# Pyramid-pooled attention in split float32: the 110 cells padded to 128 rows, probabilities normalised before the projection

## The reference

```python
qk  = relu(bn(conv1x1(x, qk_w)))      # 512 -> 256 channels
val = relu(bn(conv1x1(x, v_w)))       # 512 -> 512 channels
key, value = psp(qk), psp(val)        # adaptive max pools 1, 3, 6, 8: 110 cells
scores = softmax(query @ key * 256 ** -0.5)     # 4096 positions x 110 cells
y = scores @ value                    # 4096 x 512
out = x + bn(conv1x1(y, out_w))
```

## Time and profile before

| | us |
|---|---|
| median of the runs (3) | 1450.42 |
| the profiled execution | 1452.24 |
| its span | 1450.6 |
| TensorE matmuls busy | 1401.4 (97%) |
| VectorE busy | 967.7 (67%) |
| ScalarE busy | 434.3 (30%) |
| GpSimd busy | 438.0 (30%) |

### The profile page before, as it was taken

How to read it: one execution, slowest core, us unless ns; L and a number is a source line. 1 busy time by engine, 2 the same in 40 slices (tenths; PEclk the granted TensorE clock), 3 DMA queues, 4 the chain that set the end, 5 groups by cost and what they waited for, 6 DMA issues and landing times.

```text
span 1450.6 us, 17388 instructions
## 1 busy us (share of the span) xinstructions
PE 1401.4 (97%) x6029; PEld 1131.5 (78%) x6029; DVE 967.7 (67%) x1745; ACT 434.3 (30%) x597; POOL 438.0 (30%) x263
## 2 busy tenths in 40 slices
PE   7999999999999999999999999999999999999885
PEld 6888888888788887887788877888878887888653
DVE  6545666776666757667576776666766767766776
ACT  4112232233232232332332232332332232232241
POOL 0000123323323323323133323223223323323366
PEclk9999999999999999999999999999999999999987
DMA  5113243443443442443443442443434442442257
GB/s 189 59 58 98 77 171 120 145 174 118 143 171 118 145 172 96 166 170 120 145 145 136 154 168 93 174 163 127 145 127 149 159 174 104 157 174 91 84 205 259
DMA packets 102923, 204.60 MB, mean 141 GB/s; under 512 B 3242, under 2 KB 3282, under 8 KB 102866
## 3 DMA queue, kind: packets, MB, share of 16 engines
q1 hardware_dynamic: 102290, 202.93, 39.6%
q10 hardware_dynamic: 576, 1.05, 0.2%
HBM read 136.86 MB, written 67.11 MB: 141 GB/s over the span
## 4 chain that ended last, share of the span: by engine, by line
PE 85%; DVE 6%; issue 3%; DMA 2%; POOL 2%; ACT 1%; DVEq 0%; POOLq 0%; SPq 0%; ACTq 0%
PE conv_ps L328 22%; PE conv_ps L329 22%; PE conv_ps L330 22%; PE out_ps L352 3%; PE out_ps L353 3%; PE out_ps L354 3%; POOL xo L283 2%; PE score_ps L364 2%; PE score_ps L366 2%; PE score_ps L365 2%; DMA xo<-x 1%; DMA out<-xo 1%; DVE y L673 1%; DVE part L622 1%; PE sum_ps L341 1%
## 5 line engine op out<-in xcount | busy, mean ns | idle before, releaser
L283 POOL TENSOR_TENSOR xo<-y,xo 128x512 f32<-128x512 f32 x256 | 437.1, 1714 | 1009.3 <-DVE y L673 992.4
L328 PE MATMUL conv_ps<-xh,wh 128*128 128x512 f32 x1536 | 601.9, 392 | 0.0
L329 PE MATMUL conv_ps<-xh,wl 128*128 128x512 f32 x1536 | 600.5, 391 | 0.0
L330 PE MATMUL conv_ps<-xl,wh 128*128 128x512 f32 x1536 | 600.3, 391 | 0.0
L605 DVE TENSOR_REDUCE row_max<-conv_ps 128x64 f32<-128x512 f32 (+2 forms) x576 | 289.7, 531 | 280.3 <-ACT q L466 141.0
L328 PEld LDWEIGHTS conv_ps<-xh,wh 128*128 128x128 f32 x1536 | 289.6, 189 | 63.4
L329 PEld LDWEIGHTS conv_ps<-xh,wl 128*128 128x128 f32 x1536 | 290.1, 189 | 62.4
L330 PEld LDWEIGHTS conv_ps<-xl,wh 128*128 128x128 f32 x1536 | 289.5, 188 | 61.3
L478 ACT ACTIVATE e<-score_ps 110x512 f32<-110x512 f32 x60 | 36.1, 601 | 695.0 <-PE score_ps L366 695.0
L673 DVE TENSOR_TENSOR y<-out_ps,rsum 128x512 f32<-128x512 f32 x238 | 161.9, 684 | 1.1
L466 ACT ACTIVATE q<-conv_ps,shift 128x512 f32<-128x512 f32 x128 | 88.2, 689 | 236.6 <-PE conv_ps L330 236.6
(11 more groups left out here) (103 smaller groups left out, 806.0 us busy)
## 6 DMA issues: line engine op xcount, KB each, us to landing
xo<-x SPq DMA_DIRECT2D x64, 1024.0 KB, 5.5
xa<-x SPq DMA_DIRECT2D x63, 1024.0 KB, 7.7
out<-xo SPq DMA_DIRECT2D x63, 1024.0 KB, 4.2
q<-v_w ACTq DMA_DIRECT2D x4, 256.0 KB, 4.9
xa<-x SPq DMA_DIRECT2D x2, 512.0 KB, 6.1
q<-out_w SPq DMA_DIRECT2D x1, 1024.0 KB, 8.4
out<-xo SPq DMA_DIRECT2D x4, 256.0 KB, 2.0
q<-qk_w SPq DMA_DIRECT2D x1, 512.0 KB, 8.4
```

What stands on the lines that cost most here:

```text
L283: nc.gpsimd.tensor_tensor(xt, y[:, m % 2, :], xt, ALU.add).then_inc(out_added, 1)
L328: nc.tensor.matmul(bank(t, c)[:, :], wh[:, k, cols], hi, start=(k == 0), stop=False)
L329: nc.tensor.matmul(bank(t, c)[:, :], wl[:, k, cols], hi, start=False, stop=False)
L330: last = nc.tensor.matmul(bank(t, c)[:, :], wh[:, k, cols], lo, start=False, stop=(k == KC - 1))
```

## The change

The number of matmuls and of bytes moved stays. What differs:

- **Rows.** Keys, values, shift rows, e, sums and projections have ROWS = 128 rows in place of 110. The 18 added rows are set to zero once, by GpSimd; the matrix of ones that sums the cells has zeros in those rows.
- **Order of the arithmetic.** e is split and summed as before (low part now by GpSimd). Then e is multiplied by 1/sum on VectorE (`normalise`), split again (high part ScalarE, low part VectorE), and this p is projected. The projected blocks need no scaling, and VectorE adds the residual itself (`add_out`). The product `scale_out` and GpSimd's `add_residual` are gone. e has three buffers. GpSimd has the low parts of e and q.
- **Order of a step on TensorE.** sums, convolutions 0 to 2, projections 0 and 1, convolution 3, scores, convolution 4, projections 2 and 3, value projection, convolution 5.
- **Order on VectorE.** refine, normalise, pooling of cells, low part of p, keys; values behind the first row pooling.
- **No hardware loop**: every engine's steps are written out.
- **Tail.** Residuals of the last image go to eight places (two of xa, four of q, two of xo). Scores are computed two tiles and sums one tile ahead of the projection.

The core of the diff (on each engine `for s in range(S)` replaces `steps`; `ap = s - NT - 1`, `ac = s - NT`):

```diff
+ROWS = 128
...
-        e = sb("e", [CELLS, 2, TN])
+        e = sb("e", [ROWS, 3, TN])
...
+        def residual(a):
+            if a < LAST:
+                return xo[:, a % 2, :, :]
+            q2 = [q[:, 2 * i:2 * i + 2, :, :].rearrange("p t c n -> p (t c) n") for i in range(4)]
+            return [xa[:, 0, :, :], xa[:, 1, :, :], q2[0], q2[1], xo[:, 0, :, :], xo[:, 1, :, :], q2[2], q2[3]][a - LAST]
...
+            def split_e_lo(a):
+                pool.wait_ge(e_hi, a + 1)
...
+                nc.gpsimd.tensor_tensor(e_l[:, u, :], e[:, u, :], e_h[:, u, :], ALU.subtract).then_inc(e_lo, 1)
...
+            for s in range(S):
+                if s >= NT:
+                    split_e_lo(s - NT)
+                if s >= NT - 1:
+                    split_q_lo(s - (NT - 1))
...
+            def project(a, m):
+                if m == 0:
+                    pe.wait_ge(p_lo, a + 1)
...
+                if ap >= 0:
+                    sums(ap)
+                conv(s, 0)
+                conv(s, 1)
+                conv(s, 2)
+                if ap >= 0:
+                    project(ap, 0)
+                    project(ap, 1)
+                conv(s, 3)
+                if ac >= 0:
+                    scores(ac)
+                conv(s, 4)
+                if ap >= 0:
+                    project(ap, 2)
+                    project(ap, 3)
+                if ac >= 0 and ac % NT == 0:
+                    project_values(ac // NT)
+                conv(s, 5)
...
+            for a in range(LAST, S):
+                if a + 2 < S:
+                    scores(a + 2)
+                if a + 1 < S:
+                    sums(a + 1)
                 for m in range(OC):
+                    project(a, m)
...
+                if ap >= 0:
+                    guess(ap)
+                if s + 1 < S:
+                    split_hi(s + 1, 0)
+                if ap >= 0:
+                    split_p_hi(ap)
+                if s + 1 < S:
+                    split_hi(s + 1, 1)
...
-                nc.vector.tensor_tensor(y[:, m % 2, :], out_bank(b, t, m)[:, :], rsum[:, :], ALU.mult)\
-                    .then_inc(out_scaled, 1)
...
+            def normalise(a):
+                dve.wait_ge(rsum_ready, a + 1)
+                u = a % 3
+                nc.vector.tensor_tensor(e[:, u, :], e[:, u, :], rsum[:, :], ALU.mult).then_inc(p_made, 1)
...
+                xt = residual(a)[:, m, :]
+                nc.vector.tensor_tensor(xt, out_bank(a, m)[:, :], xt, ALU.add).then_inc(out_added, 1)
...
+                if ap >= 0:
+                    refine(ap)
+                    normalise(ap)
+                    if ap % NT == 0:
+                        values_lo(ap // NT)
+                if s >= 1:
+                    pool_cells(s - 1)
+                if ap >= 0:
+                    split_p_lo(ap)
+                if last_of_batch:
+                    finish_keys(ac // NT)
+                pool_rows(s, 0)
+                if last_of_batch:
+                    finish_values(ac // NT)
...
+            for a in range(LAST, S):
+                if a + 1 < S:
+                    refine(a + 1)
+                    normalise(a + 1)
+                add_out(a, 0)
+                add_out(a, 1)
+                if a + 1 < S:
+                    split_p_lo(a + 1)
+                add_out(a, 2)
+                add_out(a, 3)
```

More of the change, by code:

```diff
@@ L144, in psp_attention @@
         rsum_ready = sem("rsum_ready")
+        p_made = sem("p_made")
+        p_hi = sem("p_hi")
+        p_lo = sem("p_lo")
         vo_turned = sem("vo_turned")
@@ L177, in splits_q @@
[L177 to L211, removed]
+        def wait(eng, s, n):
+            if n > 0:
+                eng.wait_ge(s, n)
@@ L239, in _ @@
             sp.wait_ge(w_in[VC - 1], 16)
-            load(0, 1)
+            load(1)
             sp.dma_start(w_raw[:, CC:PAR, :], out_w.rearrange("(m p) c -> p m c", p=P)).then_inc(w_in[VC + 1], 16)
[L243 to L264, removed]
@@ new lines, in _ @@
+            sp.wait_ge(q_lo, LAST + 2)
+            load_residual(LAST + 2)
+            store(LAST - 1)
+            stored(LAST - 2)
+            load_residual(LAST + 4)
+            sp.wait_ge(q_lo, LAST + 4)
+            load_residual(LAST + 3)
+            stored(LAST - 1)
+            load_residual(LAST + 5)
+            store(LAST)
+            sp.wait_ge(q_lo, LAST + 6)
+            load_residual(LAST + 6)
+            store(LAST + 1)
+            sp.wait_ge(q_lo, LAST + 8)
+            load_residual(LAST + 7)
@@ L268, in _ @@
+            for a in range(LAST + 2, S - 1):
+                store(a)
+            for m in range(OC):
+                sp.wait_ge(out_added, (S - 1) * OC + m + 1)
+                sp.dma_start(out_v[B - 1, :, m, (NT - 1) * TN:], residual(S - 1)[:, m, :]).then_inc(y_last, 16)
+            sp.wait_ge(y_last, (NT - 1 + OC) * 16)
         @block.gpsimd
@@ L285, in step @@
[L285 to L295, removed]
+            one = e[:, 0, 0:ROWS]
+            nc.gpsimd.memset(one, 1.0).then_inc(ones_made, 1)
+            pool.wait_ge(ones_made, 1)
+            nc.gpsimd.affine_select(out=one, in_=one, compare_op=ALU.is_ge, fill=0.0, base=CELLS - 1,
+                                    pattern=[[0, ROWS]], channel_multiplier=-1).then_inc(ones_made, 1)
@@ new lines, in split_q_lo @@
+            def split_q_lo(a):
+                pool.wait_ge(q_hi, a + 1)
+                nc.gpsimd.tensor_tensor(q_l[:, a % 2, :, :], q[:, a % NT, :, :], q_h[:, a % 2, :, :], ALU.subtract)\
+                    .then_inc(q_lo, 1)
+            for s in range(S):
+                if s >= NT:
+                    split_e_lo(s - NT)
+                if s >= NT - 1:
+                    split_q_lo(s - (NT - 1))
+            split_q_lo(LAST + 1)
+            split_e_lo(LAST)
+            split_q_lo(LAST + 2)
@@ L331, in conv @@
                 last.then_inc(conv_done, 1)
-            def sums(b, t):
-                wait(pe, e_lo, b, t, 1, 1 - (NT + 1))
-                if t == 1:
-                    pe.wait_ge(vo_made, b)
-                wait(pe, s_r0_made, b, t, 1, (-1 if sum_bank(b, t) is conv_ps[1] else 0) - (NT + 1))
-                u = (t - 1) % 2
-                nc.tensor.matmul(sum_bank(b, t)[:, :], ones[:, :], e_h[:, u, :], start=True, stop=False)
-                nc.tensor.matmul(sum_bank(b, t)[:, :], ones[:, :], e_l[:, u, :], start=False, stop=True)\
-                    .then_inc(sums_done, 1)
@@ L344, in project, with scores @@
-            def project(b, t, m):
-                if m == 0 and t == 1:
-                    pe.wait_ge(vo_lo, b)
-                four = isinstance(b, int) and NT * b + t > NT * B
-                if m < 2 or four or not (isinstance(b, int) and b >= B):
-                    wait(pe, out_scaled, b, t, OC, m - (3 if four else 1) - (NT + 1) * OC)
-                cols, u = slice(m * P, (m + 1) * P), (t - 1) % 2
-                bk = out_bank(b, t, m)
+            def scores(a):
+                if a % NT == 0:
+                    pe.wait_ge(key_ready, a // NT + 1)
+                pe.wait_ge(q_lo, a + 1)
+                wait(pe, exp_done, a - 1 if a > LAST else a)
+                if a == LAST + 1:
+                    pe.wait_ge(rows_pooled, CC * S)
+                sc, u = score_bank(a)[0:ROWS, :], a % 2
+                for i in range(QC):
+                    nc.tensor.matmul(sc, key_h[:, i, :], q_h[:, u, i, :], start=(i == 0), stop=False)
+                    nc.tensor.matmul(sc, key_l[:, i, :], q_h[:, u, i, :], start=False, stop=False)
+                    last = nc.tensor.matmul(sc, key_h[:, i, :], q_l[:, u, i, :], start=False, stop=(i == QC - 1))
+                last.then_inc(scores_done, 1)
@@ new lines, in sums @@
+            def sums(a):
+                pe.wait_ge(e_lo, a + 1)
+                wait(pe, s_r0_made, a)
+                if a % NT == 0 and a < LAST:
+                    pe.wait_ge(vo_made, a // NT + 1)
+                nc.tensor.matmul(sum_ps[0:ROWS, :], ones[:, :], e_h[:, a % 3, :], start=True, stop=False)
+                nc.tensor.matmul(sum_ps[0:ROWS, :], ones[:, :], e_l[:, a % 3, :], start=False, stop=True)\
+                    .then_inc(sums_done, 1)
+            def project(a, m):
+                if m == 0:
+                    pe.wait_ge(p_lo, a + 1)
+                    if a % NT == 0:
+                        pe.wait_ge(vo_lo, a // NT + 1)
+                if a == LAST - 1 and m >= 2:
+                    pe.wait_ge(rows_pooled, CC * S)
+                else:
+                    wait(pe, out_added, OC * a + m - (3 if a >= LAST else 1))
+                bk, cols, u = out_bank(a, m), slice(m * P, (m + 1) * P), a % 3
@@ L354, in project @@
                 nc.tensor.matmul(bk[:, :], vo_h[:, cols], e_l[:, u, :], start=False, stop=True).then_inc(out_done, 1)
-            def scores(b, t):
-                if t == 0:
-                    pe.wait_ge(key_ready, b)
-                wait(pe, q_lo, b, t, 1, 1 - NT)
```

(102 more changed lines are left out.)

442 lines of the change are left out of this document (207 added, 235 removed).

## The result

The changed kernel takes 1427.53 us (median), the kernel before 1450.37 beside it: ratio 0.984, 95% interval 0.982 to 0.986. It is faster, by 22.8 us where 38 were forecast, and lies 0.5 us above the top of my range. One of its four runs was slow (1749.99 us at a granted clock of 0.75), and the median of the other three is 1426.75 us. Its profiled execution took 1426.75 us with a span of 1424.9.

A forecast was written before the change was run, and what follows sets the result against it. TensorE's matmul cadence was taken to bound the kernel up to 1361.4 us, a chain of several engines the tail behind it. 1361.4 - 15.0 - 2.7 - 11.8 = 1331.9, plus tail 81 = 1413, near 1412 us; range 1401 to 1427.

The forecast's parts named there:

- Loop gone, 15.0: Steps at the hardware loop's back edge: writing the loop out removes VectorE's issue waits, 15.0 us off.
- Late projection of the image's first step, 2.7: Six steps opening a batch image: keys moved behind the refinement remove one late projection, 6 x 0.45 = 2.7 us off.
- Padding, 11.8: Small-group matmuls in every step: with 128 rows they go at full spacing, 0.21 us per step, 11.8 us off.
- padding buys nothing: Rival, small matmuls in steps: spacing comes from switching operands, not rows; 1424 us, chance 0.22.
- columns rule: Skill's rule for TensorE matmuls: time goes by columns, contraction rows do not matter, so padding gains near 0.
- New chain of normalise and split, 0: Sums to p_lo in each step: ready at 611.3, TensorE wants it at 612.9; slack 1.6 us, 0 charged.
- The slower side: Rival, every step: GpSimd's q split delays p_lo, TensorE waits 1.0 us per step, 55 in all; 1467 us, chance 0.07.
- Tail 81: After the last convolution: 27 to first p_lo, 47 for seven VectorE turns, 2.8 adds, 3.8 end; 81 us against 89.2.
- Two smaller terms: End of the tail: last tile's adds 2.8 us, then 3.8 us from the last add to the span's end.
- the third term: The padding gain in the steps up to the last convolution, 11.8 us off.

The follow-up runs named there:

- e9_aligned: Changed kernel (128 rows) plus two unused 32-byte tiles, so every TensorE operand starts on a multiple of 128 bytes; 1416.80 us.
- e10_unpad_aligned: Changed kernel with 110 rows again and tiles started on multiples of 128 bytes by small unused tiles; 1426.94 us.

## Why the prediction was wrong, step by step

1. *Loop gone, 15.0.* Right: 15.8 measured alone, and no wait for issue on VectorE is left.
2. *Late projection of the image's first step, 2.7.* Right in size by the trace: 24.3 to 23.80, six times 0.5, or 3. It was not tried alone.
3. *Padding, 11.8.* This step failed: it was worth 0 (a plain step of 21.07, not 20.85). I took "every partial form is slower and no full one is" for a cause. Rows were one difference between the two kinds of matmul; the start of their operands on 128 bytes was another, and I had not read it. With both put right, in e9_aligned, the stretch of steps comes out as I had summed it (1331.8), so the size was right and its condition was half known. The rival "padding buys nothing" had 1424 and a chance of 0.22; its time is within 3.5 us of the result, its reason (operands changing place at the ends of groups) was nearer, but not right either, since with the same ends and other addresses the extra goes. My argument against it, that the ends could not hold 10 ns per matmul, was wrong too: behind a pair of projections eleven convolution matmuls carry 0.05 us. The columns rule of the Trainium skill ("TensorE: Matmul & The Clock Gate", LDWEIGHTS), which is stated there of the load of the weights, spoke for 0. 0 it was, but not by that rule: e9_aligned against e10_unpad_aligned shows 10 us that the 18 added rows are worth once the tiles are aligned.
4. *New chain of normalise and split, 0.* Right: TensorE is busy 1175.10 of 1175.10 us. The slack was larger than the forecast 1.6: in the step shown p_lo ends at 601.59, and TensorE takes it up at 604.36. The slower side (a split on GpSimd falling on the refinement in every step) did not come; it came in the tail, where I had priced it.
5. *Tail 81.* Right in the sum, 80.9, and in part by luck. The first tile's p_lo ended 26.5 us into it (27 forecast), and seven turns of VectorE took 45.9 (47). But a turn free of collisions and waits took 5.06 us, not 5.6, which makes 4 to 5 us less in all; the collisions came to about 7.8 (8 forecast); and VectorE waited 2.8 us once and 0.6 once for ScalarE's guess, which I had not priced. The first of these waits came behind TensorE at a granted clock of 0.52 from 1370 to 1376. Two smaller terms missed in opposite ways: after the last p_lo it took 5.4 us to the last add, not 2.8, since TensorE, at a granted clock of 0.64 from 1418 to 1421 after an idle time of 2.0 us, gave the blocks one by one; and 3.1, not 3.8, from there to the end.

The sum without the third term is 1361.4 - 15.0 - 2.7 + 81 = 1424.7, and the span is 1424.9. So with the failed term alone put at 0 the sum meets the span.

Two things more put the time just above the range. The sum started from a profiled execution that was 1.8 us slower than the median of the kernel before (1452.24 and 1450.42), and I took that off by reading the span, 1.6 us shorter than the time of its execution (1450.6), as a median. In the changed kernel the profiled execution (1426.75) is not slower than the median, so the median lies 2.6 us above the span of 1424.9. And the rival with 0.22 had a spread of some us above its 1424, while my range ended at 1427.

## What to carry to other kernels

A comparison of fast and slow instructions of one kernel shows what they differ in, not which difference counts: look for a second difference (here the start addresses) before giving the first a price, and undo each alone and both together. One tile of odd size moves all that is allocated behind it; put such tiles last, or round them up. When an instruction is held to keep it from colliding, keep its lead over its reader.

## What I had not expected of the hardware

TensorE's cadence for float32r matmuls of 512 columns depended on two things at once: 226.7 ns when all operands had 128 rows and started on 128 bytes (a step of 92 in 20.85 us), and about 0.2 us more per step (21.03 to 21.09) if either failed for the 20 small-group matmuls. The extra need not show on the instruction that causes it: with 128 rows off 128 bytes, eleven matmuls behind the projection took 2.54 us in place of 2.50. Which of the addresses matter most was tried only in part (moving operand 0.08 us of 0.11). A start 64 bytes past was not enough for e and vo, which lay there in the changed kernel and carried the 0.11.
